# Graph layers of a four-layer graph network: the bias term moves from VectorE to a one-row product on TensorE

## What is computed

```
def _L1_gnn_ref(x, edge_index, W_in, b_in, Ws, bs):
    N = x.shape[0]
    loop = jnp.arange(N, dtype=edge_index.dtype)
    src = jnp.concatenate([edge_index[0], loop])
    dst = jnp.concatenate([edge_index[1], loop])
    deg = jax.ops.segment_sum(jnp.ones_like(dst, dtype=x.dtype), dst, num_segments=N)
    dis = jax.lax.rsqrt(jnp.where(deg > 0, deg, 1.0))
    norm = dis[src] * dis[dst]
    h = x @ W_in + b_in
    for i in range(Ws.shape[0]):
        xw = h @ Ws[i]
        msg = xw[src] * norm[:, None]
        agg = jax.ops.segment_sum(msg, dst, num_segments=N) + bs[i]
        h = jax.nn.relu(agg)
    return h
...
x = _layernorm(x + _L1_gnn_ref(x, edge_index, L1_gnn_W_in, L1_gnn_b_in, L1_gnn_Ws, L1_gnn_bs), axis=-1)
```

## Time and profile before

| | us |
|---|---|
| median of 3 executions | 3914.11 |
| lowest and highest | 3901.14, 3917.30 |
| span of the profiled execution | 4181.7 |
| of it the three graph layers (1821 to 2808) | 987 |

### The profile page before, as it was taken

The page is one execution under the profiler, slowest core; times in us unless marked ns, Lnnn a source line. Parts: engine busy times, 40 slices in busy tenths (PEclk is TensorE's granted clock), DMA queues, the critical chain, the costliest instruction groups (busy, mean ns, idle before and its releaser), DMA issues. The chain is left out here.

```text
span 4181.7 us, 48029 instructions
## 1 busy us (share of the span) xinstructions
PE 2722.1 (65%) x11826; PEld 1763.4 (42%) x11826; DVE 3383.5 (81%) x7569; ACT 2541.1 (61%) x5535; POOL 2469.1 (59%) x2202
## 2 busy tenths in 40 slices
PE   3878878787860688745545543435888887676664
PEld 2555555555540344434534433422444443334442
DVE  2789999999997788837747757974999998798776
ACT  1678777787872466626535544543787777465554
POOL 6456655656620566447646646646666661778887
PEclk7999999999985777757657766656999898675555
DMA  3577876666652988637746756751332231333332
GB/s 89 133 178 197 193 190 190 186 196 190 203 171 68 255 251 253 203 101 237 239 156 221 241 189 190 230 164 43 87 85 85 79 85 45 105 98 86 89 94 64
DMA packets 402066, 644.05 MB, mean 154 GB/s; under 512 B 127455, under 2 KB 207720, under 8 KB 401790
## 3 DMA queue, kind: packets, MB, share of 16 engines
q1 hardware_dynamic: 332030, 527.96, 42.1%
q0 software_dynamic: 69760, 113.02, 11.1%
HBM read 347.78 MB, written 296.81 MB: 154 GB/s over the span
## 5 line engine op out<-in xcount | busy, mean ns | idle before, releaser
L1605 POOL DMA_INDIRECT gs_g<-table_xw,slot_idx x588 | 611.6, 1040 | 413.3 <-issue 251.7
L896 POOL DMA_INDIRECT gs_t<-table_x,slot_idx x392 | 446.4, 1139 | 369.1 <-POOLq L83 142.6
L505 POOL DMA_INDIRECT gs<-x,src_idx x200 | 221.2, 1106 | 369.6 <-DMA xd_rows<-gd 283.4
L378 PE MATMUL ps<-ident,own_g 128*128 128x128 f32 x588 | 142.1, 387 | 443.1 <-DVE own_g L1707 343.6
L1651 ACT ACTIVATE hT_g<-u_g 128x512 f32<-128x512 f32 x147 | 92.5, 629 | 460.1 <-DVE u_g L1719 279.1
L1272 POOL DMA_INDIRECT slot_idx<-node_map,src_idx x200 | 245.1, 1226 | 192.5 <-DMA slot_idx<-node_map,src_idx 86.2
L1712 DVE TENSOR_TENSOR_SCAN agg_g<-same_seg,agg_g,ps 128x512 f32<-128x512 uint8 x147 | 187.4, 1275 | 190.9 <-DMA table_x<-x_b 93.3
L378 PEld LDWEIGHTS ps<-ident,own_g 128*128 128x128 f32 x588 | 93.9, 194 | 487.1 <-DVE own_g L1707 378.1
L505 POOL DMA_INDIRECT gd<-x,dst_idx x200 | 248.0, 1240 | 60.9 <-issue 60.9
L1881 POOL DMA_INDIRECT out<-x_t,end_idx x196 | 240.7, 1228 | 66.3 <-issue 58.5
L896 POOL DMA_INDIRECT own_t<-table_x,own_idx x196 | 228.0, 1163 | 59.7 <-issue 59.7
(11 more groups left out here) (366 smaller groups left out, 9474.9 us busy)
## 6 DMA issues: line engine op xcount, KB each, us to landing
table_xw<-xw_b SPq DMA_DIRECT2D x147, 512.0 KB
table_x<-x_b SPq DMA_DIRECT2D x98, 512.0 KB
own_g<-table_xw SPq DMA_DIRECT2D x147, 256.0 KB
x_in<-x SPq DMA_DIRECT2D x49, 512.0 KB
y_g<-table_x SPq DMA_DIRECT2D x49, 512.0 KB
table_xw<-xw_g SPq DMA_DIRECT2D x98, 256.0 KB
out<-y_g SPq DMA_DIRECT2D x49, 512.0 KB
pen_t<-pen_row SPq DMA_DIRECT2D x98, 256.0 KB
```

Source lines behind the costliest of these rows:

```text
L378: last = nc.tensor.transpose(to[0:width, j * P:(j + 1) * P], t[:, j * width:(j + 1) * width], ident[:])
L505: pool.indirect_dma_start(out=to[k % 3][:, j * D:(j + 1) * D], out_offset=None, in_=x, in_offset=bass.IndirectOffsetOnAxis(ap=of[:, n:n + ...
L896: pool.indirect_dma_start(out=self.B[L % RING][g][:, t * D:(t + 1) * D], out_offset=None, in_=table, in_offset=bass.IndirectOffsetOnAxis(a ...
L1605: pool.indirect_dma_start(out=gs[c % 6][:, j * D:(j + 1) * D], out_offset=None, in_=tables[layer], in_offset=bass.IndirectOffsetOnAxis(ap= ...
```

## The change

The bias term becomes the first of the matmuls that fill `T_O`: a product of one row of `bs_row` (1 x 128, the weights) with 512 roots of degree (1 x 512, moving), over the whole bank. The own rows are then added to it by four products with the identity, each writing every fourth column of the bank, so that `T_O` stands in edge order. `agg`, `u` and `hT` are in edge order too, and the product or turn of `hT` reads every fourth column. VectorE's own-bias step goes, and its addition reads `agg` without a step. The roots come from a new table `root_row`, made in the degree stage by one ACT instruction and one DMA, and SP loads 2 KB of it per chunk.

```
-                            pe.wait_ge(S("own_bias"), SUB * (t + 1))
+                            landed(pe, "root_in", 4, t)
                             if t >= 2:
                                 pe.wait_ge(S("with_self"), t - 1)
-                            turn(pe, T_O[t % 2], own[t % 4]).then_inc(S("own_ps"), 1)
+                            nc.tensor.matmul(T_O[t % 2], bs_row[layer][0:1, :], root_e[t % 4][:], start=True, stop=False, skip_group_check=True)
+                            landed(pe, "own_in", 4, t)
+                            for j in range(SUB):
+                                last = nc.tensor.matmul(edge_order(T_O[t % 2])[:, j, :], own[t % 4][:, j * D:(j + 1) * D], ident[:],
+                                                        start=False, stop=j == SUB - 1, skip_group_check=True)
+                            last.then_inc(S("own_ps"), 1)
...
+            def edge_order(t):
+                return t.rearrange("f (p j) -> f j p", j=SUB)
...
                             sp.dma_start(own[t % 4][:], edge_rows(tables[layer], t)).then_inc(S(f"own_in{t % 4}"), 16)
+                            sp.dma_start(root_e[t % 4][:], root_row[:, t * CH:(t + 1) * CH]).then_inc(S(f"root_in{t % 4}"), 16)
...
+                                for j in range(SUB):
+                                    last = nc.tensor.matmul(T_W[c % 2][:, j * D:(j + 1) * D], cols[:, j, :], WS[layer + 1][:], start=True, stop=True)
+                                last.then_inc(S("xw_ps"), 1)
...
-                            landed(v, "own_in", 4, t)
-                            for j in range(SUB):
-                                k = t * SUB + j
-                                blk = own[t % 4][:, j * D:(j + 1) * D]
-                                V.scalar_tensor_tensor(out=blk, in0=bs_row[layer][:], scalar=root4[:, k:k + 1], in1=blk,
-                                                       op0=ALU.mult, op1=ALU.add).then_inc(S("own_bias"), 1)
...
-                            V.tensor_tensor(rows4(u[c % 2][:]), agg[c % 3].rearrange("f (p j) -> f j p", j=SUB), rows4(T_O[c % 2]), ALU.add).then_inc(S("with_self"), 1)
+                            V.tensor_tensor(u[c % 2][:], agg[c % 3][:], T_O[c % 2], ALU.add).then_inc(S("with_self"), 1)
...
+                sp.wait_ge(S("root"), 1)
+                sp.dma_start(sections(root_row), root[:]).then_inc(S("root_out"), 16)
                 sp.wait_ge(S("own_fix"), 1)
...
+                act.wait_ge(S("cnt_fix"), 1)
+                nc.scalar.activation(root[:], cnt[0:SECT, :], ACT.Sqrt, bias=1.0).then_inc(S("root"), 1)
                 act.wait_ge(S("deg4_in"), 16)
```

More of the change, by code:

```diff
@@ L92, in build @@
     cnt_row, own_row = dram("cnt_row", [1, ET]), dram("own_row", [1, ET])
+    root_row = dram("root_row", [1, ET])
     z8, a8 = dram("z8", [8, ET]), dram("a8", [8, ET])
@@ L1001, in build @@
         own = tile("own")
+        root = tile("root", W, SECT)
         own_rows = tmp.enter_context(nc.sbuf_tensor("own_rows", [TILES // 2, 2, P], F32))
@@ L1037, in _ @@
                 sp.wait_ge(S("deg4_in"), 16)
+                sp.wait_ge(S("root_out"), 16)
             @block.gpsimd
@@ L1511, in build @@
             x1_e = ring("x1_e", 8)
+            root_e = [tmp.enter_context(nc.sbuf_tensor(f"root_g{layer}_{k}", [1, CH], F32)) for k in range(4)]
             st, sd, rs, nm = (ring(n, 3, k) for n, k in (("st", 12), ("sd", 4), ("rs", 4), ("nm", 4)))
@@ L1633, in _ @@
                             pe.wait_ge(S("hT"), c + 1)
+                            cols = edge_order(hT[c % 3])
                             if last_layer:
@@ L1636, in _ @@
                                     pe.wait_ge(S("v"), c - 1)
-                                turn(pe, T_W[c % 2], hT[c % 3]).then_inc(S("h_ps"), 1)
+                                for j in range(SUB):
+                                    last = nc.tensor.transpose(T_W[c % 2][:, j * D:(j + 1) * D], cols[:, j, :], ident[:])
+                                last.then_inc(S("h_ps"), 1)
                             else:
@@ L1640, in _ @@
                                     pe.wait_ge(S("xw"), c - 1)
-                                rows_times(pe, T_W[c % 2], hT[c % 3], WS[layer + 1]).then_inc(S("xw_ps"), 1)
+                                for j in range(SUB):
+                                    last = nc.tensor.matmul(T_W[c % 2][:, j * D:(j + 1) * D], cols[:, j, :], WS[layer + 1][:], start=True, stop=True)
+                                last.then_inc(S("xw_ps"), 1)
                 @block.scalar
```

## The result

The changed kernel takes 3896.43 us (median of four runs, 3893.81 to 3898.06) beside 3914.82 us for the kernel before (3901.14 to 3917.3). The ratio is 0.9962, with a 95% interval of 0.9946 to 0.9978: 15 to 18 us less. A later comparison with 10 and 19 runs gave 3906.41 against 3918.36 us, ratio 0.9965 (0.9952 to 0.9978). The direction was forecast, the size was a half to two thirds of the 29 us, and the reason turned out to be another one.

The account below looks back on a forecast made before the run. POOL was taken as closest bound, 90% full. Chunk savings of 1.03 us times 49, 50 us, less 4 us for starts, scaled to 43 us, a third off: 29 us, 3885 us; forecast range 3865 to 3898 us, overall 3835 to 3950 us.

Parts of the forecast that it names:

- POOL as the closest bound: Graph layers: POOL's four gathers with 0.30 us lost behind each need 5.39, 5.38 and 5.36 us per chunk, 90% full.
- The sum: Three layers: 0.27 + 0.41 + 0.35 us per chunk saved, times 49, 50 us, less 4 us for starts: 46 us.
- About 0.6 us of a chunk is left: Graph layers: POOL's idle time per chunk, 0.58, 0.63 and 0.59 us, at most 88 us over three layers.
- a scaling by 0.936 and a third off: Whole program: 46 us scaled from traced span to median gives 43 us; a third off for late signals gives 29 us.
- VectorE's share: Graph layers: without the own-bias step and the addition's step VectorE needs 1.50 us less, 3.16, 3.21 and 4.01 us per chunk.
- TensorE's share: Graph layers: bias product and own products add 1.28 to 2.57 us per chunk; TensorE comes to 5.53, 5.20 and 5.09 us.
- the slower rival: Graph layers: TensorE becomes the bound if its mean clock is under 0.56 (0.61 with waits), 3970 us; slower had chance 0.20.
- The write with a step: Own products writing every fourth element of a bank: at 1.53 times, 0.47 to 0.91 us longer, 3939 us; within slower, 0.20.
- The starts and ends of the layers: Layer starts: bias and own products unhidden cost +1.4 us per layer, +4 us; ends gained some 5 us only at full gain.
- SP and the degree stage: A 2 KB load per chunk on SP, one more square root and copy in the degree stage: nothing, -0 to +1 us.
- No change: Graph layers: TensorE's late signal sets the pace, or POOL already bounds the first two; 3914 to 3898 us, chance 0.30.
- The full gain: Graph layers: all waits go, clock rises to 0.8, layers run at POOL's rate; 93 us, 3821 us, chance 0.08.

Follow-up runs that it names:

- edge_order_twice: Kernel before with own rows turned into edge order and VectorE's bias step kept, on a chip without late signals: 3910.01 us, ratio 0.9986.
- no_bias_turns_third: Changed kernel with the bias left out and own rows turned by transposes into edge order, chip without late signals: 3904.59 us, 0.9964 against the kernel before.
- before_fifth: Kernel before, unchanged, profiled again on a chip without late signals: 3920.75 beside 3918.55 us, ratio 1.0002.
- the pair of no-bias kernels: Changed kernel without the bias, on chips with late signals: own rows as products 4147.44 us (0.9934), as transposes 4145.26 us (0.9944), against the kernel before.
- after_fourth: Changed kernel, unchanged, repeated on a chip without late signals: 3906.41 us beside 3918.36 us for the kernel before, ratio 0.9965.
- the second one-row product: Changed kernel with the one-row bias product issued twice: 4068.6 us (1.0378 against the kernel before) without late signals, 4267.51 us (1.0222) with them.

## Why the prediction was right or wrong

**POOL as the closest bound: right, and understated.** "Taken up for 90%" is true of the trace that was read. In an execution like the timed ones it is 100%, before the change and after.

**The sum: the step that failed is its first term.** "About 0.6 us of a chunk is left" came from chunks of 5.97, 6.01 and 5.95 us in a trace with late signals. Without them the chunk is 263.8/49 = 5.38, 5.45 and 5.36 us before the change, and 5.33, 5.34 and 5.26 us after. What the prediction wanted to save, 0.27 to 0.41 us of idle time a chunk, wasn't there; what was saved, 0.05 to 0.11 us, is in the gathers themselves, which the prediction took as fixed at 5.39, 5.38 and 5.36 us. The text saw the danger (the trace exceeded the median by 267.6 us, and the late signal may belong to it) and answered it with a scaling by 0.936 and a third off. Neither follows from anything: if the lateness was absent, nearly all of that gain was gone, not a third. The gathers of a layer, forecast at 273 to 281 us, ran for 261.2, 261.8 and 257.7 us. That the time, 3896 us, lies inside the forecast's own 3865 to 3898 us is chance: the gain that the prediction describes didn't take place.

**VectorE's share: right.** Forecast 3.16, 3.21 and 4.01 us a chunk; 122.04/200 x 5.33 = 3.25 us, 3.25 and 4.07 us measured. The addition: 684 ns forecast, 662 measured. Worth of it on the path, though, only in the third layer.

**TensorE's share: near in its sum by two errors that cancel.** Busy per chunk: 190.14/200 x 5.33 = 5.07, 5.14 and 4.46 us against 5.53, 5.20 and 5.09. No run shows the last three, the terms that the sum starts from; the trace of the changed kernel shows 5.07, 5.14 and 4.46 us in their place. The terms are what the prediction's parts give at the granted clock of the earlier trace rows, 0.66, 0.73 and 0.62, and it was 0.85, 0.87 and 0.73. Short windows of the traces show two levels, 0.50 (2281.51 to 2283.20, the slow product of the earlier trace rows) and 1.00 (2286.30 to 2287.30, the fast one); the 0.56 of the slower rival goes by these levels. If 0.85 is seven tenths of the time at 1.00 and the rest at 0.50, the prediction's own parts give 6.32 - 0.7 x 2.95 = 4.3 us and not 5.07, an estimate. What is missing is the product of `hT`, which isn't new but reads its weights with a step of four elements now. One step at the full clock (1.00 granted from 1884.74 to 1889.20):

```profile
1884.74 0.60 PE L379 MATMUL ps<-ident,gs_g 128*128 128x128 f32 x4
1885.27 1.12 PE L1634 MATMUL ps<-root_g,bs_row 1*128 1x512 f32 x2
1886.32 1.16 PE L1637 MATMUL ps<-ident,own_g 128*128 128x128 f32 x8
1887.31 2.03 PE L1662 MATMUL ps<-WS,hT_g 128*128 128x128 f32 x8
1889.18 0.60 PE L379 MATMUL ps<-ident,gs_g 128*128 128x128 f32 x4
```

From start to start, the turn takes 0.53 us, the bias product 1.05, the own products 0.99 and the product of `hT` 1.87, where the earlier trace rows had 0.89 us for it. At the low clock it had taken 1.71 us; now it takes 1.8 to 2.1 us at either level (median from start to start 1.85 us at 0.50 and 1.86 us at 1.00), so the higher clock no longer halves it. edge_order_twice and no_bias_turns_third read `hT` in the same way and show 1.8 to 2.1 us as well. Its mean over the layers, where the next instruction starts within 2.3 us, rose from 1.50 to 1.88 us. POOL's chunk hid this, as it hid the rest. The mean of its weight loads' records went from 280 ns (before_fifth) to 329 ns. The prediction priced no part of this: "the product or turn of `hT` reads every fourth column" stands in the text ahead of it, without a term in the sum.

What the kind of instruction does to the clock isn't shown apart from its number: in the pair of no-bias kernels it is 0.79 with products and 0.66 with transposes, at 67 and 63% busy, with 807 and 688 instructions of TensorE in 240 us.

**The write with a step: next to nothing, and the sum has no term for it.** Eight instructions of the own product take 1.16 us at the full clock (row above), where a product with a contiguous output took 1.06 us in the earlier trace rows. The 1.53-fold price of that rival doesn't hold for these four-byte results: 0.1 us in 1.06. The price was real on the other side of TensorE, in the stepped read of the weights: 1.87 us against 0.89.

**The starts and ends of the layers.** +4 us were forecast; the time outside the gathers went from 65.0 us (18.2, 16.1, 30.7) to 63.4 us, and 58.0 us in after_fourth. The third layer's part of it fell from 30.7 to 27.5 and 24.9 us, and to 25.6 us with edge order alone (edge_order_twice), which fits a VectorE that is no longer behind there.

**SP and the degree stage: nothing, as costed.** TensorE waits 0.3 us (4.9 in after_fourth) for the root load in the first layer; the degree stage takes 54.2 us before and 54.7 after.

**The rivals.** "No change" was right about the chips with late signals: 1.0011 and 1.0023, by the mechanism it named in part (a shorter VectorE step only lengthens the wait), with the product's price on top. Its other half, that without late signals the first two layers are at POOL's rate already, is what the trace of before_fifth shows, for all three layers; its 3898 us was nearer than the forecast. TensorE as the bound didn't come, but it was near, with 0.25 us of a step left: the second one-row product brought it, and there TensorE set the pace at a granted clock of 0.67 and 0.72, far above the 0.56 to 0.61 from which that rival was to decide. Those figures rest on 0.89 us for the product of `hT` at the full clock, which takes 1.87. The full gain was impossible.

## What to carry to other kernels

Before a trace is taken for the time to be explained, its span must agree with the median. If it is 6% off, get a trace that agrees before pricing any idle time: here POOL's idle time ahead of its gathers was 413.3 us in one and 297.4 in the other, with nearly the same busy time (611.6 and 615.3).

Where GpSimd issues indirect transfers back to back and sets the pace, look at which VectorE instructions read two tensors from SBUF: here one that ran while a gather began could hold it until 0.87 us after its own end, as in all 107 long gathers. Taking them away is worth something even where VectorE has time to spare (here 8.6 us of gathers for 588 short instructions), and with one input from PSUM none of 482 gathers was held. In the changed kernel the addition of `y_g` and bias still costs POOL 16.6 us in this way. Moving it wasn't tried.

An engine brought to 95% looks harmless as long as another one bounds. A second product, the twin of one that took 1.13 us a step, then made the step 1.6 us longer although 0.25 us had been idle, because the clock gave way too (0.85 to 0.67, 0.5 us of a step).

When a layout changes, price each reader of it. Putting `T_O` in edge order cost 0.1 us where it is written and 0.98 us (1.87 against 0.89 at the full clock) where TensorE reads `hT` with a step as weights.

## What the runs showed of the hardware that was not expected

- **Chips differ by 6% on this program.** 3914 to 3919 us on three occasions, 4164 to 4178 us on three others, two of these on one and the same chip. By stage, before_fifth against the trace: first hop 1193.5 and 1272.6 us, attention 466.8 and 467.3, layers 858.6 and 987.1, the fourth hop 706.3 and 751.5. The attention stage is not slower. How full POOL is doesn't tell them apart: it is busy for 52% of the attention stage (1360 to 1820) and 59% of the first hop (200 to 1200), in the trace.
- **TensorE's signals on the slower kind** reach VectorE up to 28 us after the instruction's end as the trace models it, and a shorter lead of POOL cuts the longest wait at a layer's start from 19 to 28 us to 10.
- **A gather beside a VectorE instruction with two SBUF inputs** ends 0.87 us after that instruction, in 107 of 107 gathers over 1.1 us; beside anything else it took 1.00 us.
- **Weights read with a step of four elements** made the product of `hT` take 1.87 us at the full clock instead of 0.89, and 1.8 to 2.1 us over all steps, where it had been 1.71 at the low clock.
- **The clock fell when TensorE became full with products**, 0.85 to 0.67, though it had risen from 0.73 to 0.85 when it went from 59 to 95% busy. No run tells why.
